# A decoder layer on one core: query norms left in PSUM over the key blocks, and expert products of split weights

## The reference, cut to what matters

```python
# self-attention, 16 heads of 64, on (2, 1024, 256); xn is the layer norm of x
P = xn @ W_in + b_in                      # 4096 columns: q, k, v and gate of each head
d2 = q2[..., :, None] + k2[..., None, :] - 2.0 * einsum('hbtd,hbsd->hbts', Q, K)
W = power(EPS + sqrt(maximum(d2, 0.0)), -2)
W = W / (EPS + sum(W, axis=-1, keepdims=True))
x = x + (G * (W @ V)).reshape(b, t, 1024) @ W_out + b_out
# cross-attention: queries from x, 77 rows of context for keys and values (not changed)
x = x + xattn(layernorm(x), ctx, ctx, mask)
# experts: top 2 of 8 per token
y = rmsnorm(layernorm(x), rms_w)
h = silu(y @ W1[e].T) * (y @ W2[e].T)     # 256 -> 704
x = x + sum over the token's two experts of w[e] * (h @ W3[e].T)
```

## Time and profile before

| | |
|---|---|
| time, median of 3 runs | 1489.39 us (1487.73 to 1489.97) |
| profiled execution: its own time | 1485.64 us |
| profiled execution: span of the instructions | 1483.8 us |
| mean granted TensorE clock | 0.968 |
| TensorE busy | 1370.3 us (92%) |
| DVE, ACT, POOL busy | 992.5, 935.4, 606.5 us |

### The profile page before, as it was taken

How to read it: one execution, slowest core, us unless ns; L and a number is a source line. 1 busy time by engine, 2 the same in 40 slices (tenths; PEclk the granted TensorE clock), 3 DMA queues, 4 the chain that set the end, 5 groups by cost and what they waited for, 6 DMA issues and landing times.

```text
span 1483.8 us, 22919 instructions
## 1 busy us (share of the span) xinstructions
PE 1370.3 (92%) x7209; PEld 869.1 (59%) x7210; DVE 992.5 (67%) x1479; ACT 935.4 (63%) x710; POOL 606.5 (41%) x516
## 2 busy tenths in 40 slices
PE   5899999999999999999998947999974999999995
PEld 4545555555555555555554615888862666666663
DVE  7978888898888888888988564888866221221220
ACT  1789999999999999999999921333330222222221
POOL 5344454446355544644454062333321333333331
PEclk9999999999999999999999878999986999999998
DMA  5000000000000000000000033222300243313312
GB/s 150 15 1 15 29 21 21 14 28 14 17 26 28 14 14 28 21 21 14 21 14 19 9 121 116 65 64 64 122 29 15 61 113 87 90 32 87 88 34 71
DMA packets 68829, 67.25 MB, mean 45 GB/s; under 512 B 6752, under 2 KB 61280, under 8 KB 68768
## 3 DMA queue, kind: packets, MB, share of 16 engines
q1 hardware_dynamic: 61504, 56.91, 12.0%
q0 software_dynamic: 7296, 9.97, 3.9%
HBM read 49.03 MB, written 19.92 MB: 46 GB/s over the span
## 4 chain that ended last, share of the span: by engine, by line
PE 78%; DVE 9%; issue 6%; ACT 3%; DMA 2%; POOL 1%; DVEq 0%; POOLq 0%; SPq 0%; ACTq 0%
PE ps_s L568 15%; PE ps_s L838 13%; PE ps_o L583 12%; PE ps_p L471 9%; PE ps_o L863 7%; PE ps_o L660 4%; PE ps_s L471 2%; PE ps_s L693 2%; PE ps_s L721 2%; DVE wts L1042 2%; PE ps_s L515 2%; PE ps_p L596 2%; PE ps_p L851 2%; ACT wts L1549 2%; PE ps_s L507 2%
## 5 line engine op out<-in xcount | busy, mean ns | idle before, releaser
L1704 POOL TENSOR_TENSOR v_aug<-v_aug,wts 128x1024 f32<-128x1024 f32 x96 | 233.0, 2427 | 347.7 <-DVE v_aug L1031 347.3
L1042 DVE TENSOR_SCALAR wts<-ps_s,k 128x1024 f32<-128x1024 f32 x240 | 297.0, 1279 | 91.0 <-PE ps_s L568 83.2
L1543 ACT ACTIVATE wts<-wts 128x4096 f32<-128x4096 f32 (+1 forms) x80 | 230.3, 2932 | 52.4 <-DVE wts L1042 32.7
L583 PE MATMUL ps_o<-wts,head_rows 128*64 128x512 f32 x1024 | 250.2, 612 | 3.6 <-ACT wts L1551 3.6
L1549 ACT ACTIVATE wts<-wts,eps_d 128x2048 f32<-128x2048 f32 (+1 forms) x96 | 246.1, 2564 | 0.2
L1551 ACT ACTIVATE wts<-wts 128x2048 f32<-128x2048 f32 (+1 forms) x96 | 238.4, 2484 | 3.1
L1463 DVE TENSOR_TENSOR wts<-rinv,ps_s 128x352 f32<-128x352 f32 x76 | 39.6, 521 | 253.5 <-ACT rinv L1621 170.4
L838 PE MATMUL ps_s<-wts,head_rows 128*128 x608 | 197.7, 469 | 3.1 <-issue 2.2
L838 PEld LDWEIGHTS ps_s<-wts,head_rows 128*128 128x128 f32 x608 | 110.3, 191 | 64.7 <-issue 16.8
L1621 ACT ACTIVATE rinv<-ps_s 128x352 f32<-128x352 f32 x76 | 35.3, 464 | 175.8 <-PE ps_s L838 175.8
L583 PEld LDWEIGHTS ps_o<-wts,head_rows 128*64 128x64 f32 x1024 | 63.3, 137 | 120.7 <-issue 114.9
(11 more groups left out here) (241 smaller groups left out, 2348.8 us busy)
## 6 DMA issues: line engine op xcount, KB each, us to landing
wts<-in_w SPq DMA_DIRECT2D x16, 704.0 KB, 5.5
raw<-in_w_in SPq DMA_DIRECT2D x64, 128.0 KB, 2.2
h_t<-o_raw SPq DMA_DIRECT2D x16, 512.0 KB, 2.7
head_rows<-h_t SPq DMA_DIRECT2D x16, 512.0 KB, 4.3
wts<-in_w SPq DMA_DIRECT2D x8, 640.0 KB, 7.1
acc<-wts SPq DMA_DIRECT2D x17, 128.0 KB, 1.8
wts<-in_x SPq DMA_DIRECT2D x2, 1024.0 KB, 5.7
wts<-in_x SPq DMA_DIRECT2D x1, 2048.0 KB, 9.2
```

What stands on the lines that cost most here:

```text
L583: mm = pe.matmul(ps_o[r, t], v_pair[:, b, r], wts[:, h, b, t], start=b == 0, stop=b == SB - 1)
L1042: dve.tensor_scalar(wts[:, h, b, :], ps_s[:, h, :], k2[:, 2 * b + h:2 * b + h + 1], 0.0, ALU.add, ALU.max).then_inc(S_.max_ok, 1)
L1543: act.activation(chunk(start, end), chunk(start, end), ACT.Sqrt).then_inc(S_.sqrt_ok, 1)
L1704: pool.tensor_tensor(acc_w[:, 0], acc_w[:, 0], wts[:, 0, b], ALU.add).then_inc(S_.add_ok, 1)
```

## The change

Attention: the fourth product is made only for key block 0, in float32, straight from the squares `q_sq` and a constant of 0.25; for blocks 1 to 7 `start` is not set, so that a block's products are added to what `ps_s` still holds of the block before. For this the keys are stored as differences: `k_step` is the key of block 0, then key `b` minus key `b-1`. `norm_q`, `norm_rows`, `q_n` and `k_n` are gone. `copy_k` has two instructions more, and those that waited for `k_cp` on TensorE now wait for the differences (`step_ok`). POOL squares the keys ahead of the queries. One projection step moves from block 7 to block 6.

Experts: each product of `up_gate` becomes three `F32R` products. ACT writes the high parts of the next tile's weights (`high_parts`), DVE the low parts (`low_parts`), for every tile anew; the rows are split by `copy_in`. The parts lie in buffers of the attention, two sets in turn. `turn_h(i-1)` moves ahead of `up_gate(i, 0)`. In the diff, `low_parts` and the `expert_tile` at the end are DVE's.

```diff
-QK_STEPS = (0, 0, 4, 8, 12, 15, 18, 21, 24)
+QK_STEPS = (0, 0, 4, 8, 12, 15, 18, 22, 24)
...
+    c[:, C_SQ:C_SQ + P] = 0.25
...
-                    pe.wait_ge(S_.qn_ok, n + 1)
+                    pe.wait_ge(S_.max_ok, NB * n - 1)
...
             def project_v(n, keys):
-                    pe.wait_ge(S_.k_cp, keys)
+                    pe.wait_ge(S_.step_ok, keys)
...
             def distances(n, b):
-                    terms = ((k_hi[:, s_blk], q_hi), (k_hi[:, s_blk], q_lo), (k_lo[:, s_blk], q_hi), (k_n[:], q_n))
+                    terms = ((k_hi[:, s_blk], q_hi), (k_hi[:, s_blk], q_lo), (k_lo[:, s_blk], q_hi))
+                    if b == 0:
+                        terms += ((cst[:, C_SQ:C_SQ + P], q_sq(n)),)
...
-                            mm = pe.matmul(ps_s[:, h, t], k[r], q[r, t], start=i == 0, stop=i == len(terms) - 1)
+                            mm = pe.matmul(ps_s[:, h, t], k[r], q[r, t], start=b == i == 0, stop=i == len(terms) - 1,
+                                           skip_group_check=b > 0)
...
             def up_gate(i, par, j, lead):
...
+                        if j == 0:
+                            pe.wait_ge(S_.wlo_ok, 2 * DC * i + k * DC + c + 1)
+                        w_hi, w_lo = columns(W_HI[par][k * DC + c], j), columns(W_LO[par][k * DC + c], j)
+                        for n, (y, w) in enumerate(((y_hi, w_hi), (y_hi, w_lo), (y_lo, w_hi))):
+                            mm = pe.matmul(ps_s[:, k, j * HALF:j * HALF + DEH], y[:, par, c], w,
+                                           start=n == c == 0, stop=n == 2 and c == DC - 1)
...
             def copy_k(n):
+                dve.tensor_scalar(k_step[:, 0:P], src[:, 0:P], bias(1, n), None, ALU.add)
+                dve.wait_ge(S_.k_cp, n + 1)
+                dve.scalar_tensor_tensor(out=k_step[:, P:], in0=src[:, P:], scalar=bias(1, n), in1=k32[:, 0:T - P],
+                                         op0=ALU.add, op1=ALU.subtract).then_inc(S_.step_ok, 1)
...
+            def low_parts(i, par, slot, first, last):
+                for kc in range(first, last):
+                    dve.wait_ge(S_.whi_ok, 2 * DC * i + kc + 1)
+                    for a, b, hi, lo in pieces(W_HI[par][kc], W_LO[par][kc]):
+                        raw_part = w12[:, bass.ds(slot, 1), kc // DC, kc % DC, a:b].rearrange("p s n -> p (s n)")
+                        low = dve.tensor_tensor(lo, raw_part, hi.bitcast(F32), ALU.subtract)
+                    low.then_inc(S_.wlo_ok, 1)
...
             def expert_tile(i, par, n, last=False):
-                gated(i, par, 0, n)
+                if not last:
+                    slot = slot_of(i + 1)
                 if n >= 1:
                     copy_h(i - 1, 1 - par, n - 1)
+                if not last:
+                    low_parts(i + 1, 1 - par, slot, 0, DC)
+                gated(i, par, 0, n)
+                if not last:
+                    low_parts(i + 1, 1 - par, slot, DC, 2 * DC)
                 gated(i, par, 1, n)
```

More of the change, by code:

```diff
@@ L146, in program @@
         k_lo = sb("k_lo", [P, T], F32R)
-        q_n = sb("q_n", [P, T], F32R)
-        k_n = sb("k_n", [P, P], F32R)
+        k_step = sb("k_step", [P, T])
         k2 = sb("k2", [P, NB])
@@ L155, in program, with q_sq @@
         rinv = sb("rinv", [P, T])
-        q32, k32, q_sq, v_t = qk, norms, qk_sq, qk_sq
+        q32, k32, v_t = qk, norms, qk_sq
+        def q_sq(n):
+            return o_raw if isinstance(n, int) and n == 0 else qk_sq
         acc_w = v_aug[:].rearrange("p a b t -> p a (b t)")
@@ L221, in program, with whole, pieces, columns @@
         y_in = qk[:, 0:2 * D].rearrange("p (s d) -> p s d", s=2)
-        y_tt = qk[:, 2 * D:4 * D].rearrange("p (s c t) -> p s c t", s=2, c=DC)
+        y_hi, y_lo = (w[:].rearrange("p c k n -> p (c k n)").rearrange("p (s c t) -> p s c t", s=2, c=DC) for w in (wqk_hi, wqk_lo))
+        wvg_flat = [w[:].rearrange("p c h n -> p (c h n)") for w in (wvg_hi, wvg_lo)]
+        x_hi_flat, x_lo_flat = (v[:].rearrange("p c t -> p (c t)") for v in (xn_hi, xn_lo))
+        def whole(v, at=0):
+            return ((0, DE, v[:, at:at + DE]),)
+        W_HI = ([whole(x_hi_flat, kc * DE) for kc in range(2 * DC)],
+                [whole(q_hi), whole(k_hi), ((0, DEH, wvg_flat[0][:, 0:DEH]), (DEH, DE, wvg_flat[1][:, 0:DEH])), whole(x_hi_flat, 2 * DC * DE)])
+        W_LO = ([whole(x_lo_flat, kc * DE) for kc in range(2 * DC)],
+                [whole(q_lo), whole(k_lo), whole(x_lo_flat, 2 * DC * DE),
+                 ((0, DEH, x_hi_flat[:, 5 * DE:5 * DE + DEH]), (DEH, DE, x_lo_flat[:, 5 * DE:5 * DE + DEH]))])
+        def pieces(his, los):
+            cuts = sorted({a for a, _, _ in his + los} | {DE})
+            for a, b in zip(cuts, cuts[1:]):
+                hi, lo = (next(v[:, a - a0:b - a0] for a0, b0, v in parts if a0 <= a and b <= b0) for parts in (his, los))
+                yield a, b, hi, lo
+        def columns(parts, j):
+            return next(v[:, j * DEH - a:(j + 1) * DEH - a] for a, b, v in parts if a <= j * DEH and (j + 1) * DEH <= b)
         s_up = rinv[:, 0:DE]
@@ L499, in project_first @@
                     mm.then_inc((S_.q_proj, S_.k_proj)[k], 1)
[L501 to L508, removed]
             def norm_k(n, out):
@@ L831, in turn_in, with up_gate @@
                 mm.then_inc(S_.yt2_mm, 1)
-            def up_gate(i, par, j, slot, lead):
+            def up_gate(i, par, j, lead):
                 if not lead:
@@ L984, in split_low @@
                 dve.tensor_tensor(q_lo[:], q32[:], q_hi[:].bitcast(F32), ALU.subtract)
[L985 to L992, removed]
+                dve.tensor_tensor(k_lo[:], k_step[:], k_hi[:].bitcast(F32), ALU.subtract).then_inc(S_.split_ok, 1)
             def copy_k2(n):
@@ L1116, in pair @@
                 if ahead >= 1:
-                    copy_vt(p + 1, p + 3 if ahead == 2 else PAIRS)
-                if ahead == 2:
-                    norm_rows(p + 2)
-                if ahead >= 1:
+                    copy_vt(p + 1)
                     copy_g(p + 1)
@@ L1132, in _ @@
             split_low(0)
-            norm_rows(0)
             copy_k2(0)
-            copy_vt(0, 1)
+            copy_vt(0)
             for b in range(SB):
@@ L1150, in _ @@
             split_high(1)
-            norm_rows(1)
             copy_g(0)
@@ L1635, in copy_out, with slot_and_count, high_parts, expert_tile @@
                 act.activation(o_sb[:, par], ps_o[:, HALF:HALF + D], ACT.Copy, scale=w_slot[:, bass.ds(i, 1)]).then_inc(S_.o_ok2, 1)
-            def expert_tile(i, par, k, n):
-                silu(i, 0, n)
+            def slot_and_count(i):
+                return (act.value_load(tab_i[0:1, bass.ds(ET + i, 1)], min_val=0, max_val=1),
+                        act.value_load(tab_i[0:1, bass.ds(i, 1)], min_val=64, max_val=64 * E))
+            def high_parts(i, par, slot, count, first, last):
+                if first == 0:
+                    act.wait_ge(S_.e_in, count)
+                    if not (isinstance(i, int) and i <= 1):
+                        act.wait_ge(S_.ug_mm, 2 * i - 2)
+                for kc in range(first, last):
+                    for a, b, hi in W_HI[par][kc]:
+                        raw_part = w12[:, bass.ds(slot, 1), kc // DC, kc % DC, a:b].rearrange("p s n -> p (s n)")
+                        high = act.activation(hi, raw_part, ACT.Copy)
+                    high.then_inc(S_.whi_ok, 1)
+            def expert_tile(i, par, k, n, last=False):
+                if not last:
+                    slot, count = slot_and_count(i + 1)
                 if n >= 1:
                     copy_h(i - 1, 1 - par, n - 1)
+                if not last:
+                    high_parts(i + 1, 1 - par, slot, count, 0, DC)
+                silu(i, 0, n)
+                if not last:
+                    high_parts(i + 1, 1 - par, slot, count, DC, 2 * DC)
                 silu(i, 1, n)
```

75 lines of the change are left out of this document (36 added, 39 removed).

## The result

The changed kernel takes **1444.12 us** (median of 4 runs, 1443.44 to 1445.67) against 1488.64 (1487.73 to 1489.97) before: ratio **0.970, 95% interval 0.969 to 0.972**. The forecast was 1446.5. The profiled execution took 1445.67 us with a span of 1443.8, which is 40.0 less than the span of before. The medians are 44.5 apart, since the profiled run of before was 3.0 under its median, and faster than every other run of this kernel (1487.7 to 1492.1), while that of after was 1.6 over its median.

A forecast was written before the change was run, and what follows sets the result against it. TensorE alone was taken to bound the expert tiles, TensorE and ACT the attention's loop. Attention -21 and experts -22 sum to -43: 1485.64 to 1442.6 profiled, 1446.5 as a median; own range 1438 to 1456, wider range 1428 to 1466.

The forecast's parts named there:

- The loop, -11.7 for 13 pairs: Attention's loop: guard 7 starts sooner and ACT's last root ends 0.9 us earlier per pair, 13 x -0.9 = -11.7 us.
- The pair behind the loop: Attention's pair after the loop, which has no copies of keys: -1.3 us.
- Block 0, +1.26 per pair, side by side: Block 0's float32 steps on TensorE, halves of the rows side by side: +1.26 us per pair; otherwise +2.98.
- The start, -8: Start of the kernel, pairs 0 and 1: removed query norms and cheaper distances give -8 us, between -3 and -10.
- The experts, -22 (36 tiles x -0.64, first tiles +1): Expert tiles: one-pass products at 0.165 us, 7.95 us per tile in place of 8.59; -22 us, between -36 and 0.
- The term for the first tiles: First two expert tiles: they lose 1 us because weigh_slots stands behind the first low parts.
- The slack of 0.6 at `turn_h`: Expert tile: DVE ends the second gated at 7.2 us, TensorE asks at 7.8; less slack in every other tile.
- Splitting that bounds the tiles: Rival, expert tiles: slower low parts or ACT reads make tiles 8.4 us and more, experts -6, total 1462; chance 0.17.
- Products as slow as those of 512 columns: Rival, experts: 352-column one-pass products take 0.232 us, tile 9.4, experts +31, total 1499; chance 0.04.
- The chance of 0.09: Rival of a larger gain, its wording cut from the prediction's text; chance 0.09.
- the attention: The whole attention stage, loop and start together: -21 us, between -5 and -28.

The follow-up runs named there:

- Experiment 10: Changed kernel with key differences from the copied keys behind copy_vt, ACT's table reads early, pair 1's low parts ahead of copy_g: 1423.1 us, ratio 0.955.
- experiment 2: The kernel before with only the experts' half of the change: 1464.6 us, ratio 0.983.
- experiments 1: The kernel before with only the attention's half of the change: 1470.9 us, ratio 0.988.
- experiment 6: Changed kernel with ACT reading slot and count of the next expert tile twice: 1466.7 us, ratio 0.984.
- experiment 7: Changed kernel with ACT's copy_out moved behind the two table reads, so the reads come earlier: 1436.4 us, ratio 0.964.
- 11: Changed kernel with POOL's split_qk ahead of its square_q, a single run: 1445.1 us.
- experiment 4: Changed kernel without the query-norm term in block 0: 1433.3 us, with two expert tiles less because the routing differs.
- experiment 8: Changed kernel with differences behind copy_values (not pair 0), projection steps moved, pair 1's low parts ahead of copy_g, split_qk ahead of square_q, early ACT reads: 1454.4 us.

## Why the prediction was right, and where not

- **The loop, -11.7 for 13 pairs.** Right: -0.82 per pair, -10.7 in all, period 49.91 where 49.8 was forecast, by the mechanism named (guard 7 sooner, ACT's wait 0.99 where 0.9 was forecast; the gap ahead of `project_v` is 1.51, where a microsecond was). The pair behind the loop gave 1.4 (1.3 forecast). Experiment 10 shows what the differences cost there: with them behind guard 7 and behind `copy_vt`, the pair gains another 0.93.
- **Block 0, +1.26 per pair, side by side.** Right in the loop (four records in 1.03, the block 3.3 as forecast) and off its path, with 0.7 us to spare. How much slack block 0 has, the prediction had only bounded; one path of it, through `copy_q`, it hadn't seen.
- **The start, -8.** In the table it gave -4.3 (-0.2 in pair 0, -4.1 in pair 1), but this can't be read from these two traces. The trace of experiment 2 has the attention of before too, from an ordinary execution, and there the clock was granted at 0.77 where the trace of before has 1.00 (the windows below, before and then experiment 2). Its last roots of pairs 0 and 1 are at 64.69 and 120.61, in place of 62.76 and 117.60: against them the changed kernel gained 2.1 in pair 0 (1.8 forecast) and 7.3 up to pair 1 (8 forecast). With the changed attention the last root of pair 1 is anywhere from 113.14 to 115.38 (experiments 1, 6, 7, 11 and the kernel after). So the start gave between 2 and 7.5, and that the whole term was wrong is not shown.
```profile
29.00:35.00 6.00, 5.36 (x44) 4.74 (x43) 5.77 (x8) 0.00 (x0) 5.92 (x7) 1.00 0.32 90
29.00:35.00 6.00, 4.94 (x33) 4.11 (x31) 5.17 (x7) 0.00 (x0) 5.92 (x7) 0.77 0.33 88
```
- **What the start's sum left out.** Two things were missing from it all the same. It left out the 1.3 of key differences ahead of guard 7 in pair 1, which it had counted in every pair of the loop. And it left out block 0's +1.26 in pairs 0 and 1: in pair 0, `distances` 0 starts 1.9 sooner, at 29.46, but takes 5.0. Of that, 3.3 is what the block takes in the loop; the rest is the clock, granted at 0.72 in this stretch [window 29 to 35 above].
- **Between the stages.** The gain shrank from 16.5 to 14.9 there. From the last root of pair 15 to the first expert product are 308.2 before, 309.2 in experiment 2, 309.8 after, and 308.2, 309.9 and 307.5 in experiments 1, 6 and 7 with the same attention as after: this differs from run to run by 2 us, and the change has no part in it that these traces show. In the trace of after, the last read of the heads (`head_rows` from `h_t`) took 8.59 us in place of 7.06; in experiments 1 and 7 it took 6.98 and 7.02.
- **The experts, -22 (36 tiles x -0.64, first tiles +1).** The mechanism was right and the size nearly: 7.92 per tile where 7.95 was forecast, 0.160 per product where 0.165 was, and ACT's two reads 1.22 where 1.2 was (one load takes 0.28 here, not the 0.48 of the earlier trace rows; each is followed by register instructions of 0.15 at the median). It is -0.67 x 36 = -24. The term for the first tiles failed: they lost nothing (19.46 us from the first product to that of tile 2 before, 19.34 after); by which work the later `weigh_slots` is hidden wasn't tried. The slack of 0.6 at `turn_h` was really 0 in the tiles with cut pieces and 1.0 in the others.
- **The rivals.** Splitting that bounds the tiles fell as a big loss (low parts of 704 columns 0.80 apart, as forecast) but is true in small: 0.27 of the 7.92 are its doing, and experiment 6 shows that 1.2 us more of it cost 22.6 in all. Products as slow as those of 512 columns fell by the 0.160. The 0.160 is 0.012 above half a float32 record of 352 columns (0.148), where the 0.232 of 512 columns is 0.017 above its half (0.215); the prediction's 0.165 was an estimate with the same excess at both widths. The chance of 0.09 is for a larger gain: no run shows these products under 0.160, and the tile took 7.92, with early reads 7.65 (experiment 7).

The total came within 3 us of the forecast partly by luck: by the medians of experiments 1 and 2, the attention gave 2 us too few and the experts 3 too many, and the two offset each other.

## What to carry to other kernels

When a critical chain is shortened, look for the second parent of its first link: here two were less than a microsecond apart, and the second one took over. A wait made on TensorE isn't free, whether work was taken away (experiment 4) or moved (experiment 8): behind waits of 1.77 and 2.15 us the clock fell in seven and ten of thirteen periods (to 0.66 and 0.51), and the pair got longer than before the edit. In experiment 8 the cure was to bring forward what TensorE waited for, one line for 32 us. A trace is one execution: at the kernel's start, two traces of the same code were 3 us apart, as much as some of the terms to be judged. Where an engine has a wait of its own, put its reads of numbers from the table (1.22 us for two here) into it: that gave 7.7 us for a reordered call.

## What the runs showed of the hardware

- In the loop the granted clock fell behind waits of 1.77 us (to 0.66 on the mean of the next 5 us) and 2.15 us (to 0.51 over 3 us), and not in the kernels whose waits in the loop were 1.40 or 1.51. It did not fall each time: six periods of thirteen in experiment 4 and three of thirteen in experiment 8 went without, behind the same waits. At the kernel's start it was low behind shorter ones: 0.72 from 29 to 35 us in the kernel after, where TensorE waited 0.72 and then 1.43, and 0.77 in experiment 2, where it waited 1.10 and then 1.06. What decides was not tried.
- A TensorE wait of 0.17 or 1.24 us ahead of `turn_h` is followed by 0.28 us more until the first product (0.91 in place of 0.63 from the start of `turn_h`), the same after either wait; the products run as usual.
- A float32 product of 512 columns has two records and takes 0.86 us, a product of `F32R` one record and 0.232: 3.7 times. For 352 columns it is 4.93 / 8 = 0.62 against 0.160, 3.9 times. Four passes and one, as the words on the number formats have it, show in these ratios alone; the traces have no record of a pass.
- POOL's 128x256 multiplications, two in a row, take 1.19 us beside DVE instructions that read PSUM and 3.15 beside those with two SBUF inputs.
- One load from the table takes ACT 0.28 us in the tiles; two reads with their register instructions take 1.22, and with a second pair of them TensorE's wait at `turn_h` grew by 1.07, from 0.17 to 1.24 (experiment 6).
